# Layer 1's inverse norms as exp(-0.5 ln s) on ScalarE, and a two-column ln after each half of gelu in layers 0 and 1

## What is computed

```
def _l2norm(x):
    n = jnp.sqrt(jnp.sum(x * x, axis=-1, keepdims=True))
    return x / jnp.maximum(n, EPS_NORM)
...
q = _l2norm(q) * sm
k = _l2norm(k)
scores = jnp.einsum('bhqd,bhkd->bhqk', q, k)
probs = jax.nn.softmax(scores, axis=-1)
...
h = jax.nn.gelu(x2 @ fc1_w.T + fc1_b, approximate=False)
```

## Time and profile before

| | |
|---|---|
| median of three runs | 1164.77 us |
| lowest and highest | 1163.01 and 1164.93 us |
| span of the profiled execution, first to last instruction | 1160.9 us |
| PE busy | 1094.3 us, 94% |
| ACT busy | 800.4 us, 69% |
| DVE busy | 706.6 us, 61% |
| mean granted clock of PE | 0.983 |

### The profile page before, as it was taken

One profiled execution on the slowest core, in us unless ns is written; L12 is line 12 of the kernel. 1 busy time (PEld: TensorE's weight loads), 2 busy tenths in 40 slices (PEclk: granted clock), 3 DMA queues, 4 the chain that ended last, 5 costly groups with the idle time before them and its releaser, 6 DMA issues.

```text
span 1160.9 us, 19685 instructions
## 1 busy us (share of the span) xinstructions
PE 1094.3 (94%) x6717; PEld 703.3 (61%) x6717; DVE 706.6 (61%) x1484; ACT 800.4 (69%) x1336; POOL 491.9 (42%) x447
## 2 busy tenths in 40 slices
PE   8899999889898999999999999999999999999985
PEld 5576877655555565656657656566656566555442
DVE  6554447535256266234775865865865866898874
ACT  3563655477788778787687686687687686686763
POOL 3542742613543623644335553335344345254222
PEclk9999999899999999999999999999999999999997
DMA  7000001213222203321122231023031121232301
GB/s 234 20 26 28 2 10 31 62 38 94 60 64 73 75 1 82 84 58 35 28 75 73 69 83 42 15 65 82 23 88 29 39 55 51 56 84 55 83 12 36
DMA packets 36385, 64.45 MB, mean 56 GB/s; under 512 B 7208, under 2 KB 22312, under 8 KB 36288
## 3 DMA queue, kind: packets, MB, share of 16 engines
q1 hardware_dynamic: 36288, 63.20, 20.6%
HBM read 22.90 MB, written 2.12 MB: 22 GB/s over the span
## 4 chain that ended last, share of the span: by engine, by line
PE 73%; DVE 10%; ACT 8%; issue 6%; POOL 4%; POOLq 0%; ACTq 0%; DVEq 0%
PE rings L597 13%; PE AVB L709 13%; PE rings L598 11%; PE rings L599 11%; PE rings L696 10%; PE rings L671 5%; DVE m L1203 2%; PE rings L729 2%; ACT probs L891 2%; PE rings L734 2%; PE rings L640 1%; ACT L891 1%; DVE m L1183 1%; ACT gT_h L957 1%; PE rings L746 1%
## 5 line engine op out<-in xcount | busy, mean ns | idle before, releaser
L1203 DVE TENSOR_REDUCE m<-rings 128x1 fp32r<-128x512 f32 x512 | 319.0, 681 | 100.6 <-PE rings L671 73.3
L891 ACT ACTIVATE probs<-rings 128x512 f32<-128x512 f32 x562 | 292.9, 616 | 99.4 <-PE rings L671 71.1
L696 PE MATMUL rings<-SQ,SK 64*128 64x512 f32 x768 | 237.9, 446 | 14.7 <-ACT probs L888 6.3
L671 PE MATMUL rings<-SK,SQ 63*128 63x512 f32 x512 | 200.3, 457 | 5.4 <-ACT probs L891 4.2
L696 PEld LDWEIGHTS rings<-SQ,SK 64*128 64x128 f32 x768 | 109.0, 188 | 142.4 <-issue 55.1
L709 PE MATMUL AVB<-probs,V 128*32 128x512 f32 x1536 | 193.6, 611 | 0.0
L1306 POOL TENSOR_TENSOR gT_l<-gT_f,gT_h 128x512 fp32r<-128x512 f32 x96 | 121.4, 1286 | 75.7 <-ACT gT_h L957 73.8
L888 ACT ACTIVATE probs<-rings 128x1024 f32<-128x1024 f32 x103 | 101.0, 1037 | 34.2 <-PE rings L696 20.6
L597 PE MATMUL rings<-w_h,gT_h 128*128 128x256 f32 x384 | 110.2, 287 | 1.2 <-ACT gT_h L957 0.7
L671 PEld LDWEIGHTS rings<-SK,SQ 63*128 63x128 f32 x512 | 84.2, 184 | 39.7 <-ACT probs L891 33.1
L598 PE MATMUL rings<-w_l,gT_h 128*128 128x256 f32 x384 | 106.7, 278 | 0.0
(11 more groups left out here) (185 smaller groups left out, 2229.4 us busy)
## 6 DMA issues: line engine op xcount, KB each, us to landing
SQ<-qh SPq DMA_DIRECT2D x96, 128.0 KB, 2.6
SK<-kh SPq DMA_DIRECT2D x96, 128.0 KB, 2.8
SQ<-ql SPq DMA_DIRECT2D x48, 128.0 KB, 2.7
SK<-kl SPq DMA_DIRECT2D x48, 128.0 KB, 2.9
raw<-in_w SPq DMA_DIRECT2D x20, 256.0 KB, 2.8
wmod_s<-in_wmod SPq DMA_DIRECT2D x6, 512.0 KB, 4.1
gates<-gate_rows SPq DMA_DIRECT2D x12, 256.0 KB, 3.6
raw<-in_wqkv SPq DMA_DIRECT2D x9, 256.0 KB, 2.8
```

The costliest lines, as they stand in the source:

```text
L671: mm = pe.matmul(o[:, :], SQ[a % 4][r:r + KS, n // 2, c * P:(c + 1) * P], SK[a % 4][r:r + KS, n // 2, :], start=True, stop=True)
L696: mm = pe.matmul(o[:, :], SK[a % 4][r:r + KS + 1, n // 2, c * P:(c + 1) * P], SQ[a % 4][r:r + KS + 1, n // 2, :], start=True, stop=True)
L891: act.activation(probs[:, n % PROBS, :], bank(kind, a, i)[:, :], ACT.Exp, scale=SCALE[layer(unit_job(a))]).then_inc(done["scores"], 1)
L1203: nc.vector.tensor_reduce(m16[:, col:col + 1], bank(kind, a, i)[:, :], AX_X, ALU.max, negate=True).then_inc(done["max"], 1)
```

## The change

The root in `qkroot` becomes two activations, Ln and then Exp with scale -0.5, with a semaphore `logs` between them; what they leave in `rs` is the inverse norm already, so the reciprocal on DVE in `qkrs` is dropped. At the end of each half of gelu in layers 0 and 1 (jobs 0 to 7, 16 halves) ACT takes the ln of one column of a constant tile `log_one` into its other column; nothing reads the result.

```
@@ act, qkroot
                     act.wait_ge(ss_ready, nth(kind, a))
-                    act.activation(rs[:, :, :], ss[:, :, :], ACT.Sqrt).then_inc(done[kind], 1)
+                    act.activation(rs[:, :, :], ss[:, :, :], ACT.Ln).then_inc(logs, 1)
+                    act.wait_ge(logs, nth(kind, a))
+                    act.activation(rs[:, :, :], rs[:, :, :], ACT.Exp, scale=-0.5).then_inc(done[kind], 1)
@@ act, gelu, behind the loop over its four pieces
                         ins.then_inc(done["fc1"], 1)
+                    if layer(a) < 2:
+
+                        act.activation(log_one[:, 1:2], log_one[:, 0:1], ACT.Ln)
@@ dve, once at the start
+            nc.vector.memset(log_one[:, :], 1.0)
@@ dve, qkrs
                     dve.wait_ge(done["qkroot"], nth("qkroot", a))
-                    link(nc.vector.reciprocal(rs[:, :, :], rs[:, :, :]))
                     dve.wait_ge(done["headscale"], 1)
```

More of the change, by code:

```diff
@@ L369, in cond_blocks_kernel @@
         rcp = sb("rcp", [P, 2, HEADS])
+        log_one = sb("log_one", [P, 2])
         nm0, nb0, sum0, rc0 = [small[:, n, :] for small in [sb("small", [P, 4, TT])] for n in range(4)]
@@ L426, in cond_blocks_kernel @@
         final_dve = sem("final_dve")
+        logs = sem("logs")
         first_in = [sem(f"first_in{n}") for n in range(8)]
```

## The result

The changed kernel takes 1186.85 us (median of 4 runs, 1185.37 to 1187.94) against 1163.97 of the kernel before (4 runs). The ratio is 1.0198, with an interval of 1.0175 to 1.0221: slower by some 23 us. The profiled execution has a span of 1184.9 us, 24.0 more than before, and a granted clock of 0.974 instead of 0.983.

What follows compares the result with a forecast made beforehand. PE, busy for 1094.3 of 1160.9 us, was taken as the bound, so ACT's lateness costs where PE waits: 5.1 + 8.8 + 2.7 + 4 = 20.6 us on 1164.8 gives 1185, range 1173 to 1197.

Steps and rivals of the forecast that it cites:

- The price of a switch: On ACT, each small ln with its table load adds 1.48 us (1.47 to 1.61), with no drain seen.
- Layer 0, jobs 0 and 1: Behind and ahead of the gelu halves of jobs 0 and 1, PE loses 1.4, 1.1, 1.3 and 1.3: 5.1 us.
- the load stands behind ACT's wait for fc2a, so it isn't hidden: Job 1, second half of gelu: the load starts only after ACT's wait for fc2a, so PE loses 1.3 us.
- Halves with an exp behind: Gelu halves of jobs 3 to 7: four at 1.45, two at 1.4, one at 0.2, sum 8.8 us.
- Job 6's first half: Behind this gelu half, ACT's next wait of 1.27 is 0.2 less than the 1.48 added: PE loses 0.2 us.
- the places forecast at nothing: Gelu halves of job 2, first of job 3, second of jobs 4 and 5: ACT's lateness costs PE nothing.
- The root: At the four qkroot, ln, load and exp replace root and reciprocal: 0.9 in job 4, 0.6 each in jobs 5 to 7, 2.7 us.
- Clock: PE's granted clock falls behind longer waits: two to three falls of up to 1.7 us, 4 us taken (bounds 0 and 12).
- the seven that add to a standing wait: Seven new waits of PE lengthen existing ones to 2 to 3 us; none to all seven bring the clock down.
- ACT's lateness wasn't absorbed: Rival: ACT's idle time absorbs half of the sites and the clock stays, 8 us, 1173 us; chance 0.10.
- The clock didn't answer to most waits: Rival: the clock falls at most new waits, 1.7 us each, 30 us in all, 1195 us; chance 0.10.
- the second load of the pair: Rival: ln and exp share one set, so no load between them; no change, 1165 us; chance 0.05.

Runs made afterwards that it cites:

- the root alone: Changed kernel without the small ln, so only the root is ln and exp: 1167.3 against 1163.1 us for the kernel before, ratio 1.0037.
- the small ln alone: Changed kernel with square root and reciprocal put back, small ln kept at all 16 halves of gelu: 1186.56 us, ratio 1.0203 to the kernel before.
- the run with the joint set: Changed kernel with the small ln replaced at all 16 places by a load of the set holding ln and exp: 1167.05 us, ratio 1.0034.

## Why the prediction was right, and where it was off

**The price of a switch** held. The ln, taken as 0.19, took 0.20. The trace again shows no drain: in job 3 gelu starts at 312.13 and lasts 0.73, the load starts 0.02 later, and the exp stands right behind its load. The 1380 ns that the Trainium skill ("ScalarE: Activation LUTs", section "What ACT_TABLE_LOAD costs") adds would, as an estimate, have made each of the four waits above grow by about 2.9 (1.50 + 1.38), not 1.5.

**Layer 0, jobs 0 and 1**, came to 3.8 instead of 5.1. The step that failed is "the load stands behind ACT's wait for fc2a, so it isn't hidden", for job 1. ACT of the changed kernel there:

```profile
148.39 0.69 ACT L880 ACTIVATE kh<-rings,colv 128x512 fp32r<-128x512 f32 x1 [0.68 <-PE rings L601]
149.10 1.28 ACT L961 ACT_TABLE_LOAD   x1
152.59 0.69 ACT L961 ACTIVATE gT_f<-rings,colv 128x512 f32<-128x512 f32 x1 [2.21 <-PE rings L601]
```

and PE behind it:

```profile
153.91 0.51 PE L599 MATMUL rings<-postT_h,w_h 128*128 128x512 f32 x1 [1.36 <-ACT gT_h L961]
```

The load starts 0.02 after `kh`, and ACT waits only after it: the load lies wholly in the time in which ACT had nothing to do, and PE's wait is 1.36 as before, not 2.6. In job 0 gelu had no such wait ahead of it, and there the load cost its 1.4. Which of the waits of an activation stands ahead of its load decides this, and I had it the wrong way round: the code states the wait for `fc2a` first and that for `fc1` last, and the load ran ahead of the wait for `fc2a`; this place and the next fit a load behind the wait for `fc1`. The text on the kernel before has this order wrong too. Behind `fc1` a load isn't hidden. In job 2, where the product of `fc1` comes later in the ring than that of `fc2a`, ACT of the changed kernel waits first, and gelu starts only when the load has ended, at 226.46:

```profile
225.17 1.28 ACT L961 ACT_TABLE_LOAD   x1 [7.92 <-PE rings L601]
```

The trace of before could have told: in job 4's second half it has a load at 381.56 and 1.23 us of waiting behind it.

**Halves with an exp behind** came to 9.4 instead of 8.8, since each place gave the whole 1.50 rather than 1.40 to 1.45. Job 6's first half gave 0.3 for 0.2. At the places forecast at nothing the lag has no step of this size that isn't at a stretch of half clock. In job 2 PE ran at full clock where before it stood at half, came 1.4 us sooner and then waited 0.9 longer for POOL's `gT_l` (231.46 and 232.12 before).

**The root** came to 2.8 in the whole change and 2.75 alone, for 2.7. DVE of the changed kernel at job 5:

```profile
265.80 0.23 DVE L1152 TENSOR_TENSOR rs<-rs,rowh 128x64 f32<-128x64 f32 x1 [2.84 <-ACT rs L865]
```

It waits 2.84 instead of 1.22, so 1.62 longer, and has 0.95 less to do.

**Clock** was the term that was mis-sized: 4 us forecast, some 8 measured as the rest of the lag and 9.5 as PE's longer busy time. The price of one fall was right (1.7 at most, 1.5 to 1.7 where PE is busy). The number was not: six more stretches instead of two to three. The argument was that a single wait of 1.4 us at full clock has no fall behind it, and that only the seven that add to a standing wait and reach 2 to 3 us may have one. The length of the wait alone doesn't decide it: the two longest of those that grew (2.96 and 2.08) had none, while those of 1.98, 1.81 and 1.78 had one, and so had the 1.55 and 1.53 at AVB in jobs 4 and 5, which add to no standing wait.

A second way to the same number: among the 29 runs of the kernel before that were measured with the root alone, the four at a clock of 0.980 took 1165.4 us on average, the three at 0.987 took 1160.2. That is 0.74 us for each 0.001 (0.83 by a straight line through all 29), and from 0.983 to 0.974 it makes 6.7 us. With the 16.0 it gives 22.7 of the 24.0 between the two profiles. It isn't one profile alone that shows this: the six runs of the small ln alone have a mean clock of 0.974, those 29 have 0.984. Of the rest, and of two of the new stretches (386.9 and 414.3), I can't name the cause. That the remainder is the clock is therefore read from the stretches, from PE's busy time and from this slope; no run changed the clock alone.

**The rivals.** ACT's lateness wasn't absorbed: of the places forecast to cost, only one cost nothing. The clock didn't answer to most waits: six of the fourteen places that wait longer have a new fall, two new stretches stand elsewhere, and two old ones are gone. And the second load of the pair was there, as the order had shown; the run with the joint set shows that this rival named something real, worth 4.8 us to whoever asks for it, but not what this change does. The errors in layer 0 (+1.3) and in the clock (-4) had opposite signs, and the forecast started from 1164.8 where the kernel before took 1163.97 beside the changed one; part of the good agreement of 1185 with 1186.85 is such luck. The change itself was forecast at 20.6 and measured at 22.9.

## What to carry to other kernels

A load that is meant to be hidden has to be placed by the slack behind it: here the same joint set cost 4.0 us at one choice of places, gained 1.3 at another (an interval that holds nothing too), and 4.8 when it stood behind the copy that PE waits for. That two functions share a set saves nothing until the loads in the built program show it, so count them first. And where PE is above 90% busy, each microsecond that another engine adds at a place where PE already waits can cost more than itself, since PE's clock may fall behind the longer wait: here 16 us of waits came with 8 more, about 5 of them at such places.

## What the runs showed of the hardware that was not expected

- pow on POOL takes 1.04 us for 128x4 and 20.7 us for 128x128, while a subtraction of 128x512 takes 1.28 there: pow goes by the element, at about 160 ns for each column, if one draws a straight line through the two sizes (20734 - 1042 over 124).
- A table load can start before ACT's last wait has ended, and hides in it (149.10, with 2.21 us of waiting left behind it); or it comes behind that wait and hides in nothing (225.17, behind 7.92 us of waiting). In the first case the wait for `fc2a` ended last, in the second that for `fc1`.
- The time of one and the same kernel moved from 1158.6 to 1167.2 us between runs, and mostly with its granted clock (0.989 to 0.982 at these two ends); even with 12 runs against 17 to 29 the intervals here reach 1.7 to 2.6 us to either side, so an effect of 2 us can hardly be told.
